# Attention and feed-forward megakernel on one core: the last query tile of 512 is cut into two of 256

## The reference, cut to what matters

```
a = layernorm(x)
q, k, v = split(a @ w_attn.T + b_attn + 0.5 * (a @ la.T @ lb.T))      # 16 heads of 16
y = softmax(causal(q @ k.T / 4)) @ v
x = x + layernorm(y @ w_proj.T + b_proj + 0.5 * lora(y))
h = layernorm(x)
for blk in range(3):
    z = layernorm(qlora(h, 2 * blk)) * gamma + beta
    h = h + qlora(gelu(z), 2 * blk + 1)                               # erf gelu
x = x + layernorm(h)
```

## Time and profile before

| what | value |
|---|---|
| median of three executions | 1272.06 us |
| the profiled execution's own time | 1270.7 us |
| its span, first to last instruction | 1269.0 us |
| mean granted TensorE clock | 0.989 |
| PE busy | 96% of the span |
| ACT busy | 87% |
| DVE busy | 60% |
| POOL busy | 35% |
| chain that ended last | PE 68%, ACT 7%, DVE 6% |

### The profile page before, as it was taken

One profiled execution on the slowest core, in us unless ns is written; L12 is line 12 of the kernel. 1 busy time (PEld: TensorE's weight loads), 2 busy tenths in 40 slices (PEclk: granted clock), 3 DMA queues, 4 the chain that ended last, 5 costly groups with the idle time before them and its releaser, 6 DMA issues.

```text
span 1269.0 us, 30124 instructions
## 1 busy us (share of the span) xinstructions
PE 1214.9 (96%) x11429; PEld 526.0 (41%) x11429; DVE 764.6 (60%) x1867; ACT 1103.6 (87%) x1263; POOL 439.3 (35%) x1397
## 2 busy tenths in 40 slices
PE   8999999999999999999999999999999999999866
PEld 6556434343343434434433343333334333342255
DVE  6775226567755765786565775765766564640076
ACT  4665999999999999999999998999899999999633
POOL 3221235433433553355234344342233422220053
PEclk9999999999999999999999999999899999999979
DMA  5985644645434544444444244453434343320000
GB/s 173 317 303 176 185 121 127 189 142 144 127 117 122 154 112 124 125 121 144 122 132 133 78 139 116 113 144 90 126 117 129 112 125 96 103 85 24 5 1 17
DMA packets 144208, 159.48 MB, mean 126 GB/s; under 512 B 76326, under 2 KB 106044, under 8 KB 144060
## 3 DMA queue, kind: packets, MB, share of 16 engines
q1 hardware_dynamic: 139772, 153.26, 40.9%
q10 hardware_dynamic: 4288, 4.26, 1.1%
HBM read 117.62 MB, written 35.65 MB: 121 GB/s over the span
## 4 chain that ended last, share of the span: by engine, by line
PE 68%; ACT 7%; DVE 6%; issue 3%; DMA 3%; POOL 2%; SPq 2%; ACTq 0%; DVEq 0%
PE O L1496 30%; PE S L1478 21%; PE F L209 15%; ACT probs L1421 6%; SPq L595 1%; DMA feed_mem<-turns 1%; DMA qkv_mem<-turns 1%; PE S L1567 1%; DVE stC L1590 1%; DVE feed_mem L1697 0%; DVE o_turned L1646 0%; DVE tmpC L1607 0%; DVE feed_mem L1714 0%; DVE feed_mem L1698 0%; PE S L1565 0%
## 5 line engine op out<-in xcount | busy, mean ns | idle before, releaser
L1421 ACT ACTIVATE probs<-S 128x1024 f32<-128x1024 f32 x1056 | 995.3, 1050 | 65.2 <-PE S L1478 56.3
L1496 PE MATMUL O<-probs,vg 128*32 128x512 f32 (+3 forms) x4608 | 524.3, 565 | 4.7 <-DVE o_turned L1646 3.8
L1478 PE MATMUL S<-q_op,k_op 64*128 64x512 f32 (+3 forms) x2304 | 384.4, 425 | 9.6 <-ACT probs L1421 7.6
L1478 PEld LDWEIGHTS S<-q_op,k_op 64*128 64x128 f32 x2304 | 186.5, 184 | 324.3 <-ACT probs L1421 235.1
L1496 PEld LDWEIGHTS O<-probs,vg 128*32 128x32 f32 x4608 | 120.4, 109 | 207.9 <-issue 178.8
L1399 POOL TENSOR_SCALAR_AFFINE_SELECT probs<-probs 128x512 f32<-128x512 f32 (+1 forms) x160 | 92.1, 585 | 165.1 <-ACT probs L1421 164.5
L1372 POOL TENSOR_SCALAR tmpC<-mvC 128x2 f32<-128x2 f32 x84 | 25.7, 306 | 310.0 <-DVE rstdC L1599 308.2
L209 PE MATMUL F<-wfT,feed_mem 128*32 128x256 f32 x1280 | 81.8, 382 | 3.5 <-DMA feed_mem<-turns 1.9
L1646 DVE STREAM_TRANSPOSE o_turned<-O 128x512 f32<-128x512 f32 x32 | 22.8, 712 | 100.6 <-PE O L1496 99.6
L1698 DVE SCALAR_TENSOR_TENSOR feed_mem<-feed_mem 128x512 f32<-128x512 f32 x90 | 66.3, 737 | 3.1
L1697 DVE SCALAR_TENSOR_TENSOR feed_mem<-feed_mem 128x512 f32<-128x512 f32 x90 | 63.5, 706 | 3.5 <-DVE qkv_mem L1703 0.5
(11 more groups left out here) (207 smaller groups left out, 1288.4 us busy)
## 6 DMA issues: line engine op xcount, KB each, us to landing
k_op<-qk_rows SPq DMA_DIRECT2D x256, 256.0 KB, 3.6
qk_rows<-parts SPq DMA_DIRECT2D x32, 512.0 KB, 4.6
q_op<-qk_rows SPq DMA_DIRECT2D x128, 128.0 KB, 2.9
turns<-feed_mem SPq DMA_DIRECT2D x160, 64.0 KB, 1.9
feed_mem<-turns SPq DMA_DIRECT2D x40, 256.0 KB, 2.9
k_op<-qk_rows SPq DMA_DIRECT2D x48, 128.0 KB, 2.6
x_in<-in_L_attn_x ACTq DMA_DIRECT2D x8, 512.0 KB, 5.1
feed_mem<-in_L_attn_x SPq DMA_DIRECT2D x16, 256.0 KB, 3.4
```

The costliest lines, as they stand in the source:

```text
L1421: nc.scalar.activation(probs[:, n % NP, :, :], S[:, n % NS, :, :], ACT.Exp, scale=SCALE).then_inc(exp_ok, 1)
L1478: last = nc.tensor.matmul(S[:, n % NS, a, at:at + TT - q0], k_op[mine, c % RING, pair, k0:k0 + P], q_op[mine, v % QS, pair, q0:TT], start= ...
L1496: last = nc.tensor.matmul(O[h * STRIP:(h + 1) * STRIP, q0:TT], vg[:, kb, col:col + STRIP], probs[:, n % NP, a, at:at + TT - q0], start=fir ...
```

## The change

The last tile of 512 becomes two of 256, t = 7 (tokens 3584 to 3839) and t = 8 (3840 to 4095), so QT = 9 tiles. Both get four visits each, and the keys are loaded again for each visit. A key block of such a tile is one unit: both pairs of heads side by side with 256 columns each, four weight loads and four matmuls. Tile 7 has 30 units in a visit and tile 8 has 32, one of each visit being half as wide. Tile 7 goes through the ordinary feed as one half of 256 (`parted` is 1) in lane 2. Only tile 8 goes through the last feed, in two streams of 128 that share lane 0's buffers and use `S` banks only. In the last feed the scaling moves from ACT to DVE, and the root becomes one power instruction on POOL followed by one Newton round on DVE. Once all scores are issued, `weigh` goes before everything else on PE.

```diff
+QT = NT + 1
+def wide(t):
+    return TT if t < NT - 1 else TT // 2
+def tok0(t):
+    return t * TT if t < NT else t * TT - TT // 2
-VISITS = [(t, i) for i in range(NG) for t in range(2)] + [(t, i) for t in range(2, NT) for i in range(NG)]
+VISITS = [(t, i) for i in range(NG) for t in range(2)] + [(t, i) for t in range(2, QT) for i in range(NG)]
+def key_blocks(t, s):
+    if s < min(t, NT - 1):
+        return tuple(range(NB))
+    if t < NT - 1:
+        return DIAG_ORDER
+    first = tok0(t) // P - s * NB
+    return (first, first + 1) + tuple(range(first))
 def units_of():
...
-        d = kb - t * NB
-        if d <= 0:
+        d = kb - tok0(t) // P
+        if wide(t) < TT:
+            unit([(b, pair, pair * (wide(t) - q0)) for pair in range(PAIRS)])
+        elif d <= 0:
...
 def lane(t, k):
-    return (0, LANES, 1, LANES + 1)[k] if t == NT - 1 else (2 * t + k) % LANES
+    return (0, LANES)[k] if t == QT - 1 else (2 * t + k) % LANES
 def parted(t):
-    return 4 if t == NT - 1 else 2
+    return 1 if t == NT - 1 else 2
+LAST_AFTER = (NT - 2, 0)
 def runs_on(name, t, k):
-    if t == NT - 1 and name.startswith(("norm", "copy", "sc")):
+    if t == QT - 1 and name.startswith("copy"):
         return "ACT"
-    if t == NT - 1 and k % 2 and (name.startswith("rs") or name in ("add_x", "result")):
+    if t == QT - 1 and name.startswith("rs"):
         return "POOL"
 def plan():
-        due.update({x: FEED_FROM + FEED_EACH * (t + n / len(mine)) for n, x in enumerate(mine)})
+        due.update({x: FEED_FROM + FEED_EACH * (t + n / len(mine) / (1 if t < NT - 1 else 2)) for n, x in enumerate(mine)})
...
             if x[0] == "weigh":
-                return 0.5 if backlog >= BACKLOG else 2
+                return -1 if scores == NUNIT else 0.5 if backlog >= BACKLOG else 2
 def bank(name, t, k):
-            return (F, O)[other] if k == 0 else S[:, k - 1, other, :]
+            return S[:, k, other, :]
 # POOL, root, last tile
-                    for n in range(3):
-                        link(s, nc.gpsimd.tensor_scalar(w, r, r, v, ALU.mult, ALU.mult))
-                        link(s, nc.gpsimd.tensor_scalar(r, w, 1.5, r, ALU.add, ALU.mult))
-                    return nc.gpsimd.tensor_scalar(nmr[:, b], mv[:, b, 0], -1.0, r, ALU.mult, ALU.mult)
+                    return nc.gpsimd.tensor_tensor(r, r, minus_half[:, :], ALU.pow)
 # PE, score
-                            last = nc.tensor.matmul(S[:, n % NS, a, at:at + TT - q0], k_op[mine, c % RING, pair, k0:k0 + P],
-                                                    q_op[mine, v % QS, pair, q0:TT], start=True, stop=True)
+                            last = nc.tensor.matmul(S[:, n % NS, a, at:at + wide(t) - q0], k_op[mine, c % RING, pair, k0:k0 + P],
+                                                    q_op[mine, v % QS, pair, q0:wide(t)], start=True, stop=True)
 # DVE, moments and the scaling, last tile
-                        link(s, nc.vector.tensor_scalar(tmp[:, 1, b], mv[:, b, 1], -0.5, -0.5 * EPS, ALU.mult, ALU.add))
-                        return nc.vector.tensor_scalar(rstd[:, b].bitcast(I32), tmp[:, 1, b].bitcast(I32), -0.5, HALVED_SEED, ALU.mult, ALU.add)
+                        nc.vector.tensor_scalar(tmp[:, 1, b], mv[:, b, 1], -0.5, -0.5 * EPS, ALU.mult, ALU.add)
+                        return nc.vector.tensor_scalar(rstd[:, b], mv[:, b, 1], EPS, None, ALU.add)
+                def refine(s, b):
+                    r, w, v = rstd[:, b], tmp[:, 0, b], tmp[:, 1, b]
+                    link(s, nc.vector.tensor_scalar(w, r, r, v, ALU.mult, ALU.mult))
+                    link(s, nc.vector.tensor_scalar(r, w, 1.5, r, ALU.add, ALU.mult))
+                    elif t == QT - 1 and name.startswith(("norm", "sc")):
...
+                        refine(s, b)
+                        nc.vector.tensor_scalar(own(y, t, k)[:, 0, :], (xt if name == "norm_x" else normed(name, t, k))[:, 0, :], mv[:, b, 0], rstd[:, b],
+                                                ALU.subtract, ALU.mult).then_inc(dve_ok[s], 1)
```

More of the change, by code:

```diff
@@ L808 @@
 NUNIT = len(UNITS)
+UNIT_COLS = [max(at + wide(BLOCKS[b][1]) - BLOCKS[b][4] for b, _, at in parts) for parts in UNITS]
 READY = {b: max(WHERE[b, h][0] for h in range(HG)) for b in range(NBLK)}
@@ L1056, in way_left @@
         return ahead_of[x]
-    left = {x: way_left(x) for x in after if len(x) > 2 and x[1] == NT - 1}
+    left = {x: way_left(x) for x in after if len(x) > 2 and x[1] == QT - 1}
     ready = {e: {} for e in ("PE", "DVE", "ACT", "POOL", "SP")}
@@ L1071, in shape_of @@
     def shape_of(x):
-        return "score" if x[0] == "score" else "full" if x[0].startswith("turn") or len(x) == 4 and x[1] == NT - 1 else "strips"
+        return "score" if x[0] == "score" else "full" if x[0].startswith("turn") or len(x) == 4 and x[1] == QT - 1 else "strips"
     def switch(x):
@@ L1159, in attend_and_feed @@
     order, _ = plan()
-    parts_after = [{name: after for name, _, _, after in parts_of(t)} for t in range(NT)]
+    parts_after = [{name: after for name, _, _, after in parts_of(t)} for t in range(QT)]
     def lane_of(x):
@@ L1285, in stored_before @@
             s, _, _ = place_in(t, k)
-            many = sum(lane(*x) == s for x in halves if (x[0] < NT - 1 if t == NT - 1 else x < (t, k)))
+            many = sum(lane(*x) == s for x in halves if (x[0] < QT - 1 if t == QT - 1 else x < (t, k)))
             if many:
@@ L1438, in _ @@
                         last.then_inc(gelu_ok, 1)
-                    elif name.startswith(("norm", "sc")):
-                        inputs_done(act, name, t, k)
-                        if name == "sc_att":
-                            stored_before(act, t, k)
-                        src = xC[:, t % 2, rows(t, k), :] if name == "norm_x" else normed(name, t, k)
-                        b = slots(t, k)
-                        last = nc.scalar.activation(own(y, t, k)[:, 0, :], src[:, 0, :], ACT.Identity, bias=nmr[:, b], scale=rstd[:, b])
-                        last.then_inc(act_ok[lane(t, k)], 1)
                     else:
@@ L1549, in _ @@
                         o, c = divmod(n, NC)
-                        wide = at.stop - at.start
-                        last = product(into[:, o * wide:(o + 1) * wide], g["wfT"][:, 2 * m + 1, c, o * P:(o + 1) * P],
+                        many = at.stop - at.start
+                        last = product(into[:, o * many:(o + 1) * many], g["wfT"][:, 2 * m + 1, c, o * P:(o + 1) * P],
                                                 own_t(zT, t, k)[:, c, :], start=(c == 0), stop=(c == NC - 1))
@@ L1716, in _ @@
                         last.then_inc(dve_ok[s], 1)
-                    elif t == NT - 1 and name in ("add_x", "result"):
+                    elif t == QT - 1 and name in ("add_x", "result"):
                         nc.vector.tensor_tensor(xt if name == "add_x" else own(y, t, k), own(y, t, k), xt, ALU.add).then_inc(dve_ok[s], 1)
```

192 lines of the change are left out of this document (98 added, 94 removed).

## The result

The change makes the kernel slower. The median of five runs is 1281.1 us (1278.7 to 1282.69) against 1270.0 for the kernel before (1269.12 to 1274.13): ratio 1.0072, 95% interval 1.0054 to 1.009. The forecast was 1261 us. The profiled execution took 1278.7 us, its span 1276.3 us.

The account below looks back on a forecast made before the run. The prediction took ACT's Exps to pace the feedless last visit, with PE's feed work partly hidden, and a tail with each engine partly idle. Attention + 11, hand-over - 4.1 and tail - 18.3 gave 1261 us, 11 less than before; range 1246 to 1284.

Parts of the forecast that it names:

- the ring: Attention stage: key chunks asked for three ahead, some 22 us, hide the doubled key loads, priced at 0.
- The weight loads: Attention stage: twice the weight loads per score column cost PE 0.037 us a unit, 9.2 us; bounds 0 to 36.
- The feed of half (7, 0): Attention stage: tile 7's feed now runs during tile 8's visits, putting 11.8 us of products before the last Exp.
- the price of 0.5: Attention stage: each us of the 21 us added PE work lengthens the stage by 0.5 us, 10.5 us in all.
- The empty 10 us of the last visit: Last tile's fourth visit: ACT sets the pace, so PE has some 10 us free to take half the added work.
- The hand-over: Last Exp to the tail's first product: weigh first and narrower tiles cut 9.2 us to 5.1.
- The tail: First product to end: 34.7 us one stream, 2 second stream, 4 clock, 5 half (7, 0); 45.7 against 64.0.
- Half (7, 0), priced at 5: Tail: the third block of tile 7's feed collides on DVE and needs another table; 5 us, from 1 to 12.
- The one or two additional table loads: Tail: half (7, 0)'s Tanh needs another table than Gelu, one or two loads of 1.28 us, partly on the path.
- Rival 1: Half (7, 0) ends last, or its late DMAs delay the streams through fixed queues: time 1272, no change; chance 0.18.
- Rival 2: Tiles 7 and 8: weight loads exposed, PE full, last Exp 30 to 48 us later, time 1281 to 1297; chance 0.13.
- Rival 4: Tail norms: POOL's power takes 1.9 us instead of 0.4, six on the path, + 9 us, 1270; chance 0.07.

Follow-up runs that it names:

- the other side: Kernel before with twice the key loads for its last tile, the extra ones sent to spare DRAM, against the kernel before: 1283.27 us, ratio 1.0095.
- one pair of runs: Changed kernel without tile 7's feed, set against the changed kernel: 1265.45 us; stretch 9.2 us less for 12.2 us less of feed products.
- 1.1 by the other: Changed kernel with half the key loads, set against the kernel before: 1265.35 us; stretch 12.0 us longer for 10.5 us more of feed products.
- three constants: Planner's prices for key loads, query loads and gets raised: 1263.12 us in the kernel before, 1265.3 us in the changed kernel.

## Why the prediction was wrong

**The step that failed** is the last paragraph on the attention stage: "SP issues the key loads at twice the rate [...]. Chunks are asked for three ahead, some 22 us; I price them at 0, hidden by the ring." The ring does hide them: no engine waited for keys. The step asked only who waits for the keys, and not who waits behind them on SP's queue and on the DMA engines. Measured, the extra loads cost 14.0 us of the stretch (the run with half the key loads against the kernel after) and 0.0125 of the ratio, 15.9 us of time; from the other side 12.1 and 13.3 us. This holds for the order that the old plan wrote. The forecast missed the last Exp by 15.8 us. "If that cover fails ACT waits a few us for each" was not the way it went: the cover held, and the waits came elsewhere, at the gets and the feed's products behind them.

**The weight loads** (9.2 us of PE) were over-sized: 0.91 us for three units of the new shape against 0.905 of the old, by the medians of 49 and 46 batches. The three diagonal units of the earlier trace rows, from which I took 0.037 us a unit, have four matmuls each of 128, 256 and 384 columns, as many columns in sum as twelve of 256, and took 1.01 us; what made them slower no run shows. The Trainium skill ("TensorE: Matmul & The Clock Gate", section on LDWEIGHTS) gives a load as its columns / 1.2 ns, 107 ns for 128 columns; one after another, twelve would then take 1.28 us, an estimate. Here each of the twelve loads at 1107.65 lasts 183 to 190 ns, and yet all twelve with their matmuls take 0.91 us: the loads are longer than the page's figure, and they overlap. The measurement decides.

**The feed of half (7, 0)** added 10.5 us of products, 11.8 were forecast. The first evacuation came at 1100.95 (forecast 1105.5), the third block's at 1209.30, 108.4 us later, as for half (6, 0) in the earlier trace rows. But the price of 0.5 for each microsecond was too low: 0.75 by one pair of runs, 1.1 by the other. The empty 10 us of the last visit were not there to take them: ACT now has many small waits (0.34 to 0.36 us behind batches of three units). Why they come wasn't tested. The two errors, the weight loads too dear and the price too low, offset each other: with half the key loads the last Exp is at 1208.8, 2.0 us from the forecast 1206.8. That is luck, a coincidence of terms and not a proof of them.

**Visits** were forecast at 31 and 30 us; they were 33.0, 29.7, 35.0, 31.8 and 37.8, 32.7, 31.5, 31.2. They aren't equal in work: the one of 37.8 us has 568 matmuls, that of 31.5 us 438. The forecast also counted 124 units for tile 7, whose four visits have 4 x 30 = 120; that they ended at 1089.5, near the forecast 1088, is luck too, because each unit took longer.

**The hand-over** was right: 5.1 forecast, 5.13 measured.

**The tail** was 48.5 us, 45.7 forecast. The power takes 0.55 to 0.57 us (once 0.93), not 0.4, and scaling from PSUM 0.54 instead of 0.41; six norms give 0.9 us. Half (7, 0), priced at 5, moved the tail by 0.7. But 0.7 is a difference of two effects. With it the streams' fourth norm began 11.7 us after the third instead of 9.0, and the last step of products, at a clock of 1.00 instead of 0.64, was 1.7 us shorter.

Without (7, 0) the forecast has 34.7 + 2 + 4 = 40.7 us, and the tail took 47.9. Its chain shows where the missing 7.2 us are. The six norms, with what the second stream adds, take 20.3 us on it, where 15.5 + 2 = 17.5 were forecast: 2.8 more, of which the longer norm is 0.9 and the second stream the rest. All else, the products, turns and Gelus at a low clock and the store, takes 27.6 us against 19.2 + 4 = 23.2: 4.4 more. The clock has at least a part in that, by the 1.7 us of the one step; the rest isn't split. The one or two additional table loads didn't come.

**The rivals.** Rival 1 (half (7, 0) last) was wrong by 15 us: the result at 1251.34. It did name a late DMA that holds others up through fixed queues, but in the tail only. Rival 2 (the last Exp 30 to 48 us later) came near the measured 26.8 us for a reason that isn't there; it is refuted by the batches of scores above. One of its signs, a last Exp after 1217, came true all the same, so it was a sign of more than this rival. Rival 4 is refuted, 0.57 us against 1.9. No rival named the queue of SP in the attention stage, though the trace before already had DVE waiting 6.6 us for gets and some 32.6 us of SP's time in the stretch went into issuing 48 key DMAs (48 x 0.68, an estimate from 2.72 us for four); 112 of them make 76.

## What to carry to other kernels

Halving a tile doubles every load that is made once for each tile. Ask not only whether the doubled load is in time, but what is queued behind it on the issuing engine, and who waits for that, in a kernel whose engines work through fixed orders. And where a planner writes the order, compare its prices with the trace first: three constants were worth 8 us in the kernel before and 14 to 16 in the changed one, without any restructuring. The best kernel here keeps the one large tile and takes only the prices and the new tail (1258.26 us).

## What the hardware showed

- A wait of PE cost more than itself here. After 1.83 us without work a window of 4 us had a granted clock of 0.67, and 24 matmuls took 2.79 us; where the wait was 0.51 us and the clock 1.00, the same 24 took 1.50. Over the stretch, 7.5 us more of idle time came with a clock of 0.97 instead of 1.00 and with 6.5 us more of busy time for the same matmuls.
- In the tail the same 19 matmuls took 3.07 us at a granted clock of 1.00 and 4.73 at 0.64.
- The weight loads of 64 rows last 183 to 190 ns each, but twelve of them with their matmuls take 0.91 us, no more than six loads with matmuls of twice the width (0.905).
- A transfer's landing went with what else was moved: the same 256 KB gets took 3.3 us at a DMA share of 0.29 and 3.9 at 0.51, the 64 KB puts 1.8 and 2.6. A key load of four DMAs took SP 2.72 us to issue in both kernels (981.17 before, 1017.70 after), in places more.
- Of the gain of leaving out half the key loads, 5.4 us of 14.0 came with half the bytes alone, and 8.6 with half the issues at the same busy share of the DMA engines. The Trainium skill ("Trainium Kernel Development and Optimization", section Key Constraints) says that DMAs of all queues share the same 16 engines, and that issuing from several engines saves only the sequencer's issue time. The runs agree that issue time and the engines' load are costs of their own; whether a second issuing queue would bring the 8.6 us no run here shows.
- The power of a 128x1 tile on POOL took 0.55 to 0.57 us, once 0.93.
